# Local layers: feed forward's first product in fp32r parts, and norms without a power

## The chip, the cores and the metric

The kernel runs on one core of a Trainium2 chip. The metric is the device time of one execution in microseconds (us). The core's engines are named as the profile names them: PE (TensorE), ACT (ScalarE), DVE (VectorE), POOL (GpSimd) and SP (SyncE, which here only issues DMAs). Each runs its own list of instructions in order, and they wait for one another on semaphores.

## The reference, cut to what matters

The reference has four parts: an attention with relative positions, six local layers, a second attention, and a mixture of experts. The change touches the six local layers. A batch has 16 sequences of 256 tokens with 128 channels, and per layer this is computed (after the first 64 channels are kept and the other 64 are shifted by one token):

```python
qkv = x @ Wqkv                       # 16 heads of 64
q = q / max(norm(q), 1e-12) * q_scale;  k likewise
q, k = rotary(q, k)                  # cos, sin and a scale for each position
out = local_attention(q, k, v)       # windows of 32 tokens, QK_SCALE 8
x = out @ Wo + x
xn = (x - mu) / sqrt(var + 1e-5) * g + bln     # on the shifted x
a, gate = split(xn @ W1 + b1)        # W1 is 128 x 682
x = (a * gelu(gate)) @ W2 + b2 + x
```

## The kernel before

The local layers are one block of five instruction lists (lines 1253 to 2106). For each layer and each sequence there is a pass (`one_pass`) of four steps, numbered 0 to 3; a step is 128 tokens and eight heads (`s % 2` chooses the tokens, `s // 2` the heads). 6 layers x 16 sequences are 96 passes and 384 steps. The lists are software pipelined by hand. In step j of pass n:

- PE projects q and k of step j+4 (`project_qk`), transposes the normed q and k of step j+2 (`turn_qk`), projects v of j+4, transposes outputs (`turn_outputs`, L1579) and probabilities (`turn_probs`, L1593), computes the scores of j+2 (L1612), multiplies by Wo (L1631) and by the values (L1641).
- ACT does the exponentials of step j+1 (L1821), writes the mask into the score banks (L1825), squares q and k of j+4 (L1798), and copies transposed tiles out of PSUM.
- DVE multiplies q and k of j+4 by the rotation tables (L1943 to L1945, `t_done`), sums the squares (L1950), subtracts the maxima from the scores (L1966, `sub_done`), then takes the floor of the sums (L1956, `floor_done`), and norms the outputs.
- POOL runs `normalise_rows`: it adds the two halves of the rotation (L1416), raises the 128x16 sums to -0.5 (L1420), and multiplies (L1427, `qk_done`).

The feed forward of the sequence before, f = n - 1, is laid into the same pass. In step 0 DVE takes its moments and POOL its deviations (`deviations`, L1433 to L1438, between the power and the multiplication of step 0). At the end of step 1 PE transposes the normed input (`turn_xn`, L1652) and ACT applies gain and shift to it (`turned_xn`, L1837). In step 2 PE runs `first_gates` just behind `project_v`, and `last_gate_and_value` behind the scores; in step 3 it runs `first_values`. Each of the three is a call of `through_w1` (L1658): two chunks of W1 as stationary operand, at most 128 columns of it, with the 256 tokens moving. These products are in fp32, which the trace shows as two instructions each; the products with Wqkv are already in fp32r, three products of rounded parts for one.

POOL also prepares what the passes need: after `normalise_rows` of step 1 it splits the x of the sequence after the next into two rounded parts (`split_x`, L1444 and L1447, for `turn_x`), and in the last passes of a layer it makes the low parts of the next Wqkv (`low_part`, L1410). In `first_gates` PE waits for `xnT_done`, which ACT raises at L1837. A table of ACT functions is loaded twice a pass: for Gelu in step 2 (a Gelu of one column, L1793, makes the load come early), and for Exp in step 3 (L1821).

Of the kernel before, what the change touches and what calls it, by code (L numbers as in the profile page):

```python
# [18 lines left out]
F32 = mybir.dt.float32  # L19
# [6 lines left out]
P = 128  # L26
# [31 lines left out]
def shape_constants():  # L58
# [39 lines left out]
    c["rot_cos"] = lay(cos * scale * f(8), cos * inv)  # L98
    c["rot_sin"] = lay(sin * scale * f(8), sin * inv)
# [32 lines left out]
def build_program(nc, T, out):  # L132
    ctx = ExitStack()
    with ctx:
# [106 lines left out]
        with ExitStack() as st:  # L241
# [42 lines left out]
            ev_wr, tabs = sem("a_ev_wr"), sem("a_tabs")  # L284
# [6 lines left out]
            ROW, EXT, PRODUCT, PP, CHAIN = 2, 3, 4, 5, 6  # L291
            E_HIGH, E_LOW, EK_MASKED, EK_HIGH, EK_LOW = 6, 7, 8, 9, 11

            x_copied, queries_ok = sem("a_x_copied"), sem("a_queries_ok")
            far = sem("a_far")
# [6 lines left out]
            with nc.Block() as block:  # L302
                @block.sync
                def _(sp):
# [6 lines left out]
                    for name, t in (("L0_attn_Ek", 1), ("L0_attn_Eq", 2)):  # L311
# [12 lines left out]
                    sp.dma_start(tab_ext.rearrange("t d r -> d t r"), ext[:, 0:2, :]).then_inc(tabs, 16)  # L324
                    sp.wait_ge(tabs, 16)
                    sp.dma_start(ek_row, bass.AP(tab_ext, HD * NREX + KREV,
                                                 [[0, P // HD], [NREX, HD], [1, KJ]])).then_inc(tabs, 16)
                    sp.dma_start(eq_tab[:, :], bass.AP(tab_ext, 0, [[1, LB], [NREX, HD], [1, TABW]])).then_inc(tabs, 16)
                    sp.wait_ge(tabs, 16 * 3)
# [3 lines left out]
                def _(act):  # L333
# [6 lines left out]
                    for t in range(LT):  # L340
                        act.dma_start(e_col[:, t:t + 1], bass.AP(T["L0_attn_Eq"].tensor, t * (NREL - 1) * HD,
                                                                 [[0, P // HD], [1, HD], [1, 1]]),
                                      allow_slow_non_contiguous=True).then_inc(far, 16)
                        row = (1 - t) * (NREL - 1)
                        act.dma_start(ev_far[:, t, :], T["L0_attn_Ev"][row:row + 1, :].broadcast_to((P, HD))
                                      ).then_inc(far, 16)
# [8 lines left out]
                def _(pool):  # L355
# [11 lines left out]
                    pool.wait_ge(far, 16 * 2 * LT)  # L367
# [7 lines left out]
                    pool.wait_ge(ld_w, 48)  # L375
# [7 lines left out]
                    pool.wait_ge(tabs, 16 * 3)  # L383
# [773 lines left out]
        with ExitStack() as st:  # L1157
# [9 lines left out]
            w1 = sb(st, "b_w1", [P, 2 * FF])  # L1167
            w2 = sb(st, "b_w2", [P, 3, D])
# [8 lines left out]
            rnorm = sb(st, "b_rnorm", [P, 2, 16])  # L1177
            t1, t2 = sb(st, "b_t1", [P, 2, 16, BD]), sb(st, "b_t2", [P, 2, 16, BD])
# [45 lines left out]
            masked = sem("b_masked")  # L1224

            N_WA, N_LN, N_W1, N_W2 = 3, 2, 5, 3
            SEQ = 4
# [29 lines left out]
            with nc.Block() as block:  # L1257
# [148 lines left out]
                def _(pool):  # L1406
# [6 lines left out]
                    def normalise_rows(n, s, deviations_of=None):  # L1413
# [17 lines left out]
                    def deviations(f):  # L1431
# [6 lines left out]
                        nc.gpsimd.tensor_tensor(shift[:, :], less_mean[:, :], frstd[:, :], ALU.mult).then_inc(shift_done, 1)  # L1438

# [20 lines left out]
                    def one_pass(l, b, front=True, ffn=True, last_front=False, new_front=False, x_follows=True,  # L1460
                                 last_norm=False):
# [24 lines left out]
                    nc.gpsimd.memset(zero[:, :], 0.0)  # L1486
                    nc.gpsimd.memset(ss_floor[:, :, :, 1], 1e-24).then_inc(filled, 1)
# [11 lines left out]
                    one_pass(0, 1, last_norm=True)  # L1499
                    for l in range(DEPTH - 1):  # L1500
# [5 lines left out]
                        one_pass(l + 1, 1)  # L1506
# [4 lines left out]
                    deviations(DEPTH * B - 1)  # L1511

                @block.tensor
                def _(pe):
# [24 lines left out]
                    def by_high(r, s, i, new_layer):  # L1539
                        hg, ts = s % SEQ // 2, slice(s % 2 * P, s % 2 * P + P)  # L1540
                        if new_layer is not None and s % 2 == 0:

                            pe.wait_ge(w_low, new_layer * 6 + (3 * hg + i + 1))
# [216 lines left out]
                def _(act):  # L1760
                    def load_projections(l):

                        act.wait_ge(w_low, l * 6)
# [58 lines left out]

                    def mask(s):
# [22 lines left out]
                    def one_pass(part, l, b, x_follows=True, ffn=True, last_front=False, new_ffn=None):  # L1846
# [45 lines left out]
                    act.wait_ge(c_ld, 96)  # L1892
                    one_pass("first", 0, 0, ffn=False)
# [964 lines left out]
```

## Time and profile before

| | us |
|---|---|
| median of three runs (5007.28 to 5029.31) | 5020.37 |
| the profiled execution | 5004.04 |
| its span | 5002.2 |
| PE busy | 4560.0 (91%) |
| PE weight loads busy | 3754.4 (75%) |
| DVE busy | 3696.6 (74%) |
| ACT busy | 3399.6 (68%) |
| POOL busy | 3558.5 (71%) |
| mean granted clock of PE, share of full speed | 0.972 |

The span runs from the first to the last instruction. The local layers fill it from about 970 us to 4230 us. A busy share is an average over parts of the kernel with different limits, so the order of events inside one pass says more than the share.

### The profile page before, as it was taken

What the parts mean: (1) busy time and instruction counts of PE and PEld (TensorE: products, weight loads), DVE (VectorE), ACT (ScalarE), POOL (GpSimd) and SP (SyncE); (2) the same over time, 40 slices, a digit from 0 to 9 for tenths busy, and PEclk for the clock granted to TensorE, in tenths of its full rate; (3) what the DMA queues carried; (4) which work ended last, traced back from release to release, by engine and by line L of the source; (5) the groups of instructions that cost most, each with busy time, mean ns of one, the idle gap of its engine ahead of it and who ended that gap; (6) DMA issues with size and microseconds to landing.
All of it is one profiled execution on the core that took longest, in us unless ns stands there. A gap on an engine that the chain in (4) does not pass through costs nothing. (4 is left out here: it accounts for less than half of the span.)

```text
span 5002.2 us, 202509 instructions
## 1 busy us (share of the span) xinstructions
PE 4560.0 (91%) x82160; PEld 3754.4 (75%) x82160; DVE 3696.6 (74%) x7406; ACT 3399.6 (68%) x6468; POOL 3558.5 (71%) x2507
## 2 busy tenths in 40 slices
PE   6888888799999999999999999999999997888879
PEld 4777777678887888788877887888877885555557
DVE  4877777788887888778877888788877884555544
ACT  3565565577777777777777777777777774666664
POOL 3334334499999999989999999999999995222212
PEclk8999999999999999999999999999999998999889
DMA  4333333332223222332223222322232221000000
GB/s 119 98 101 112 98 104 105 93 84 69 68 69 88 70 68 69 73 83 69 69 72 85 70 69 70 87 69 70 68 74 70 69 68 40 1 0 0 0 1 18
DMA packets 500471, 338.98 MB, mean 68 GB/s; under 512 B 222559, under 2 KB 489084, under 8 KB 499213
## 3 DMA queue, kind: packets, MB, share of 16 engines
q1 hardware_dynamic: 493566, 320.55, 25.3%
q10 hardware_dynamic: 6544, 13.18, 0.9%
q8 instruction: 280, 4.59, 0.4%
q14 instruction: 81, 0.66, 0.0%
HBM read 60.06 MB, written 54.58 MB: 23 GB/s over the span
## 5 line engine op out<-in xcount | busy, mean ns | idle before, releaser
L1420 POOL TENSOR_TENSOR b_rnorm<-b_ss,neghalf 128x16 f32<-128x16 f32 x384 | 1118.2, 2912 | 25.1 <-DVE b_ss L1956 21.5
L1416 POOL TENSOR_TENSOR b_rot<-b_t 128x1024 f32<-128x1024 f32 x384 | 909.5, 2369 | 75.3 <-DVE b_t L1945 74.6
L1943 DVE TENSOR_TENSOR b_t<-psum,b_cosg 128x1024 f32<-128x1024 f32 x384 | 469.6, 1223 | 426.3 <-ACT b_sq L1798 420.3
L1427 POOL TENSOR_TENSOR b_qk<-b_rot,b_rnorm 128x1024 f32<-128x1024 f32 x384 | 731.0, 1904 | 42.8 <-POOL b_rnorm L1420 2.7
L1544 PE MATMUL psum<-b_w_hi,b_xT_parts 128*128 128x512 f32 x1152 | 528.0, 458 | 28.6 <-issue 19.3
L1798 ACT ACTIVATE b_sq<-psum 128x1024 f32<-128x1024 f32 x384 | 392.1, 1021 | 221.9 <-PE psum L1549 221.5
L1950 DVE TENSOR_REDUCE b_ss_floor<-b_sq 128x16 f32<-128x1024 f32 x384 | 464.3, 1209 | 0.0
L1549 PE MATMUL psum<-b_w_hi,b_xT_parts 128*128 128x512 f32 x1152 | 459.9, 399 | 0.0
L1545 PE MATMUL psum<-b_w_lo,b_xT_parts 128*128 128x512 f32 x1152 | 457.3, 397 | 0.0
L1631 PE MATMUL psum<-shared,b_oT 128*128 128x128 f32 x3072 | 425.2, 281 | 0.8 <-ACT b_oT L1816 0.8
L1533 PE MATMUL psum<-ident,b_qk 128*128 128x128 f32 x3072 | 405.9, 275 | 21.3 <-DVE b_o L1982 15.3
L1533 PEld LDWEIGHTS psum<-ident,b_qk 128*128 128x128 f32 x3072 | 360.0, 142 | 84.9 <-DVE b_o L1982 25.7
L1631 PEld LDWEIGHTS psum<-shared,b_oT 128*128 128x128 f32 x3072 | 380.0, 191 | 27.2 <-issue 1.5
L1821 ACT ACTIVATE b_pr<-b_pr 128x512 f32<-128x512 f32 x384 | 241.6, 629 | 217.0 <-DVE b_pr L1966 197.2
L1982 DVE TENSOR_TENSOR b_o<-psum,b_rs 128x256 f32<-128x256 f32 x768 | 326.2, 425 | 26.5
L1641 PE MATMUL psum<-b_v_win,b_prT 64*32 64x65 f32 x24576 | 336.4, 225 | 3.9 <-issue 3.8
L1612 PE MATMUL psum<-b_kT,b_qTs 64*32 64x64 f32 x24576 | 333.3, 224 | 0.4 <-issue 0.4
L1658 PE MATMUL psum<-b_xnT,b_w 128*128 128x256 f32 (+1 forms) x1152 | 306.2, 388 | 16.8 <-DVE b_hid L2006 2.9
L1612 PEld LDWEIGHTS psum<-b_kT,b_qTs 64*32 64x32 f32 x24576 | 270.6, 105 | 61.5 <-issue 49.4
L1641 PEld LDWEIGHTS psum<-b_v_win,b_prT 64*32 64x32 f32 x24576 | 272.1, 105 | 51.5 <-issue 5.0
L1816 ACT COPY b_oT<-psum 128x512 f32<-128x512 f32 x384 | 232.5, 605 | 112.6 <-PE psum L1579 112.5
L2357 ACT ACTIVATE c_probs<-psum,c_nmax 128x256 f32<-128x256 f32 x512 | 200.9, 482 | 117.5 <-DVE c_nmax L2424 117.2
(271 smaller groups left out, 11545.8 us busy)
## 6 DMA issues: line engine op xcount, KB each, us to landing
b_v_win<-b_v SPq DMA_DIRECT2D x2304, 65.0 KB
keyed<-shared SPq DMA_DIRECT2D x64, 768.0 KB, 4.7
b_v_win<-b_v SPq DMA_DIRECT2D x1152, 32.5 KB
a_logits<-keyed SPq DMA_DIRECT2D x128, 160.0 KB, 3.1
oa<-XR SPq DMA_DIRECT2D x1024, 2.0 KB
xcur<-X SPq DMA_DIRECT2D x111, 128.0 KB, 4.3
shared<-in_L_ffn_Wqkv_dram ACTq DMA_DIRECT2D x6, 1536.0 KB
a_logits<-keyed SPq DMA_DIRECT2D x64, 128.0 KB, 3.0
```

The source lines that it names most:

```text
L1416: nc.gpsimd.tensor_tensor(rot[:, i, :, :], t1[:, i, :, :], t2[:, i, :, :], ALU.add).then_inc(rot_done, 1)
L1420: nc.gpsimd.tensor_tensor(rnorm[:, i, :], ss[:, i, :], neghalf[:, :], ALU.pow).then_inc(rn_done, 1)
L1427: nc.gpsimd.tensor_tensor(qk[:, i, :, :], rot[:, i, :, :], rnorm[:, i, :, None].broadcast_to((P, 16, BD)), ALU.mult).then_inc(qk_done, 1)
L1533: last = nc.tensor.transpose(r[:, p * P:(p + 1) * P], qk[:, s % 2, a * 8 + 2 * p:a * 8 + 2 * p + 2, :].rearrange("p h d -> p (h d)"), iden ...
L1544: nc.tensor.matmul(r, xT_hi[:, ts], w_hi[:, piece(hg, i)], start=True, stop=False)
L1545: nc.tensor.matmul(r, xT_hi[:, ts], w_lo[:, piece(hg, i)], start=False, stop=False)
L1549: return nc.tensor.matmul(r, xT_lo[:, ts], w_hi[:, piece(hg, i)], start=False, stop=True)
L1612: last = nc.tensor.matmul(bank[3 + j][qs, p * 2 * WIN:(p + 1) * 2 * WIN], qTs[at, p, qs], kT[at, p, keys], start=False, stop=(p == 3), ski ...
L1631: last = nc.tensor.matmul(bank_c[:, 0:D], oT[:, p, :], wo[:, 4 * (s % SEQ // 2) + p, :], start=(p == 0), stop=(p == 3))
L1641: last = nc.tensor.matmul(r[qs, p * (BD + 1):(p + 1) * (BD + 1)], prT[at, p, qs], v_win[at, s % NV, c, p, :], start=(p == 0), stop=(p == 3 ...
L1943: nc.vector.tensor_tensor(t14, x4, tab(cosg, slice(0, BD), BD), ALU.mult)
L1950: nc.vector.tensor_reduce(ss_floor[:, t, :, 0], sq[:, :].rearrange("p (h d) -> p h d", d=BD), AX.X, ALU.add).then_inc(ss_done, 1)
```

## The change

Four edits go together.

1. `through_w1` multiplies in fp32r: W1 is split into `w1_hi` and `w1_lo`, the normed input into `xn_parts[0]` (high) and `xn_parts[1]` (low), and each chunk is hi x hi + lo x hi + hi x low. A last chunk of 85 columns is computed as 86.
2. The parts are made thus. ACT writes the high part beside `xnT` in `turned_xn`, a second 128x256 activation. POOL subtracts it for the low part (`split_xn`), at the head of step 2, before that step's `normalise_rows`, and PE waits for it (`xn_split`) in `first_gates`. W1 is split once a layer on POOL (`split_w1`) behind `split_x` in step 1 of the second pass of the layer.
3. The power at L1420 goes. ACT takes the logarithm of the sums and the exponential of -0.5 times it (`guess_norms`, between the exponentials and the mask). POOL makes one Newton step of it: four tensor_tensors of 128x16, each behind the one before. The factor 0.5 is in the rotation tables.
4. ACT preloads a table set that has both functions, in step 3 of each pass; some semaphores of the set-up are merged.

```diff
@@ constants
-    c["rot_cos"] = lay(cos * scale * f(8), cos * inv)
-    c["rot_sin"] = lay(sin * scale * f(8), sin * inv)
+    c["rot_cos"] = lay(cos * scale * f(4), cos * inv * f(0.5))
+    c["rot_sin"] = lay(sin * scale * f(4), sin * inv * f(0.5))
@@ POOL, normalise_rows
-                        pool.wait_ge(floor_done, m)
-                        nc.gpsimd.tensor_tensor(rnorm[:, i, :], ss[:, i, :], neghalf[:, :],
-                                                ALU.pow).then_inc(rn_done, 1)
+                        pool.wait_ge(guess_done, 2 * m)
+                        nc.gpsimd.tensor_tensor(rn_step[:, i, :], ss[:, i, :], rn_guess[:, i, :], ALU.mult).then_inc(step_done, 1)
+                        pool.wait_ge(step_done, 3 * m - 2)
+                        nc.gpsimd.tensor_tensor(rn_step[:, i, :], rn_step[:, i, :], rn_guess[:, i, :], ALU.mult).then_inc(step_done, 1)
+                        pool.wait_ge(step_done, 3 * m - 1)
+                        nc.gpsimd.tensor_tensor(rn_step[:, i, :], three[:, :], rn_step[:, i, :], ALU.subtract).then_inc(step_done, 1)
+                        pool.wait_ge(step_done, 3 * m)
+                        nc.gpsimd.tensor_tensor(rnorm[:, i, :], rn_step[:, i, :], rn_guess[:, i, :], ALU.mult).then_inc(rn_done, 1)
@@ POOL, new
+                    def split_xn(f):
+                        pool.wait_ge(xnT_done, 2 * f + 2)
+                        nc.gpsimd.tensor_tensor(xn_parts[:, 1, :], xnT[:, :], xn_parts[:, 0, :].bitcast(F32),
+                                                ALU.subtract).then_inc(xn_split, 1)
+
+                    def split_w1(l):
+
+                        both = slice(0, 2 * FF)
+                        pool.wait_ge(w1_ld, (l + 1) * (16 * N_W1))
+                        nc.gpsimd.tensor_tensor(w1_hi[:, both], w1[:, :], ones[:, 0:1].broadcast_to((P, 2 * FF)),
+                                                ALU.mult).then_inc(w_low, 1)
+                        pool.wait_ge(w_low, l * N_LOW + 7)
+                        nc.gpsimd.tensor_tensor(w1_lo[:, both], w1[:, :], w1_hi[:, both].bitcast(F32),
+                                                ALU.subtract).then_inc(w_low, 1)
@@ POOL, one_pass
                         for s in range(SEQ):
+                            if ffn and s == 2:
+                                split_xn(n - 1)
                             if front:
                                 normalise_rows(n + 1, s, n - 1 if ffn and s == 0 else None)
                             if last_front and s == 0:
                                 layer_gains(l + 1)
                             if x_follows and s == 1:
                                 split_x(n + 2)
+                            if new_ffn and s == 1:
+                                split_w1(l)
@@ PE
-                            last = nc.tensor.matmul(ffn_bank[0:w, j * S:(j + 1) * S], w1[:, k:k + w], xnT[:, :],
-                                                    start=(j == 0), stop=(j == 1), skip_group_check=True)
+                            w += w % 2
+                            for i, (weight, part) in enumerate(((w1_hi, 0), (w1_lo, 0), (w1_hi, 1))):
+                                last = nc.tensor.matmul(ffn_bank[0:w, j * S:(j + 1) * S], weight[:, k:k + w],
+                                                        xn_parts[:, part, :], start=(j == 0 and i == 0),
+                                                        stop=(j == 1 and i == 2), skip_group_check=True)
@@ PE, first_gates
-                            pe.wait_ge(w1_ld, (new_ffn + 1) * (16 * N_W1))
-                        pe.wait_ge(xnT_done, f + 1)
+                            pe.wait_ge(w_low, (new_ffn + 1) * N_LOW)
+                        pe.wait_ge(xn_split, f + 1)
@@ ACT
+                    def guess_norms(s, m):
+
+                        i = s % 2
+                        act.wait_ge(floor_done, m)
+                        nc.scalar.activation(log_ss[:, i, :], ss[:, i, :], ACT.Ln).then_inc(guess_done, 1)
+                        act.wait_ge(guess_done, 2 * m - 1)
+                        nc.scalar.activation(rn_guess[:, i, :], log_ss[:, i, :], ACT.Exp, scale=-0.5).then_inc(guess_done, 1)
@@ ACT, turned_xn
                         nc.scalar.activation(xnT[:, :], ffn_bank[:, 0:S], ACT.Identity, bias=lnb[:, 0:1],
                                              scale=lng[:, 0:1]).then_inc(xnT_done, 1)
+                        nc.scalar.activation(xn_parts[:, 0, :], ffn_bank[:, 0:S], ACT.Identity, bias=lnb[:, 0:1],
+                                             scale=lng[:, 0:1]).then_inc(xnT_done, 1)
@@ ACT, one_pass
+                            if j == 3 and ffn:
+                                nc.scalar.preload_act_table_set(LOG_EXP)
                             if ok(j + 1):
                                 exps(j + 1, m + 1)
+                            if ok(j + 3):
+                                guess_norms(j + 3, m + 3)
```

## Rows read from the trace of the kernel before

**Rows 1.** Busy time of each engine in a steady stretch: PE, weight loads, DVE, ACT, POOL, clock, DMA.

```profile
2200.00:2300.00 100.00, 97.81 (x2034) 82.05 (x2033) 81.74 (x177) 75.46 (x131) 94.42 (x55) 1.00 0.28 69
```

**Rows 2.** Timeline of PE, end of step 1 and step 2: start, us, engine, line, operands.

```profile
2222.00 0.44 PE L1652 MATMUL psum<-ident,b_xn 128*128 128x128 f32 x2
...
2225.25 1.03 PE L1658 MATMUL psum<-b_xnT,b_w 128*128 128x256 f32 x4
2226.52 0.66 PE L1579 MATMUL psum<-ident,b_o 128*128 128x128 f32 x4 [0.24 <-ACT b_qTs L1785]
2227.01 0.81 PE L1593 MATMUL psum<-ident,b_pr 128*128 128x128 f32 x4
2227.76 0.86 PE L1612 MATMUL psum<-b_kT,b_qTs 64*32 64x64 f32 x64
2228.75 1.09 PE L1658 MATMUL psum<-b_xnT,b_w 128*85 128x256 f32 x4
...
2231.46 0.50 PE L1544 MATMUL psum<-b_w_hi,b_xT_parts 128*128 128x512 f32 x1
```

**Rows 3.** Timeline of DVE, rotation of step 1 and floor of its sums.

```profile
2219.59 0.68 DVE L1945 TENSOR_TENSOR b_t<-psum,b_sing 128x512 f32<-128x512 f32 x1
...
2222.64 0.17 DVE L1956 TENSOR_REDUCE b_ss<-b_ss_floor 128x16 f32<-128x32 f32 x1
```

**Rows 4.** Timeline of POOL in the same stretch.

```profile
2219.02 0.19 POOL L1438 TENSOR_TENSOR b_shift<-b_less_mean,b_frstd 128x2 f32<-128x2 f32 x1
2219.17 1.90 POOL L1427 TENSOR_TENSOR b_qk<-b_rot,b_rnorm 128x1024 f32<-128x1024 f32 x1
2221.03 2.38 POOL L1416 TENSOR_TENSOR b_rot<-b_t 128x1024 f32<-128x1024 f32 x1
2223.36 2.92 POOL L1420 TENSOR_TENSOR b_rnorm<-b_ss,neghalf 128x16 f32<-128x16 f32 x1
2226.42 1.90 POOL L1427 TENSOR_TENSOR b_qk<-b_rot,b_rnorm 128x1024 f32<-128x1024 f32 x1
2228.28 0.61 POOL L1444 TENSOR_TENSOR b_x_parts<-xcur,ones 128x256 fp32r<-128x256 f32 x1
2228.97 0.73 POOL L1447 TENSOR_TENSOR b_x_parts<-xcur,b_x_parts 128x256 fp32r<-128x256 f32 x1
```

**Rows 5.** Timeline of ACT in the same stretch.

```profile
2222.48 0.56 ACT L1837 ACTIVATE b_xnT<-psum,b_lnb,b_lng 128x256 f32<-128x256 f32 x1 [1.56 <-PE psum L1652]
2222.94 0.62 ACT L1821 ACTIVATE b_pr<-b_pr 128x512 f32<-128x512 f32 x1
2223.58 1.28 ACT L1793 ACT_TABLE_LOAD   x1
2224.87 0.20 ACT L1793 ACTIVATE b_no_gate<-ones 128x1 f32<-128x1 f32 x1
```

**Rows 6.** Timeline of PE in the first attention: fp32r products of 256 columns.

```profile
500.94 0.28 PE L654 MATMUL psum<-a_k_diag,a_e_parts 128*128 128x256 f32 x1
501.06 0.28 PE L650 MATMUL psum<-a_k_diag,a_q_parts 128*128 128x256 f32 x1
```

**Rows 7.** Timeline of PE: stalls at L1652, idle time in brackets; first, third and last of eight.

```profile
1514.53 0.41 PE L1652 MATMUL psum<-ident,b_xn 128*128 128x128 f32 x2 [4.24 <-ACT b_xn L1832]
...
2154.25 0.69 PE L1652 MATMUL psum<-ident,b_xn 128*128 128x128 f32 x2 [3.50 <-ACT b_xn L1832]
...
4192.60 0.41 PE L1652 MATMUL psum<-ident,b_xn 128*128 128x128 f32 x2 [2.50 <-ACT b_xn L1832]
```

**Rows 8.** Busy time and granted clock (last but two) around these three stalls.

```profile
1513.00:1523.00 10.00, 8.47 (x100) 7.11 (x101) 4.35 (x6) 8.08 (x15) 9.78 (x7) 0.83 0.35 87
2150.00:2160.00 10.00, 6.50 (x82) 5.16 (x80) 6.93 (x19) 4.69 (x8) 7.91 (x7) 0.67 0.33 82
...
4190.00:4200.00 10.00, 6.74 (x100) 5.31 (x90) 2.77 (x11) 5.53 (x10) 1.19 (x4) 0.83 0.38 75
```

**Rows 9.** Waits of PE: who waited for whom, us in total, times, longest.

```profile
PE psum L1652 <- ACT b_xn L1832: 41.7, 19, 7.6
```

More of the change, by code:

```diff
@@ L283, in build_program @@
             ld_x, ld_c, ld_w, ld_e = sem("a_ld_x"), sem("a_ld_c"), sem("a_ld_w"), sem("a_ld_e")
-            ev_wr, tabs = sem("a_ev_wr"), sem("a_tabs")
+            ev_wr = sem("a_ev_wr")
             ev_row = k_blk[0:1, :, :].rearrange("p h l -> p (h l)")[:, 0:NREX * HD]
@@ L291, in build_program @@
             ROW, EXT, PRODUCT, PP, CHAIN = 2, 3, 4, 5, 6
+            TURNED, TABLES = 4, 6
             E_HIGH, E_LOW, EK_MASKED, EK_HIGH, EK_LOW = 6, 7, 8, 9, 11
             x_copied, queries_ok = sem("a_x_copied"), sem("a_queries_ok")
-            far = sem("a_far")
             def window_blocks(mt, hh):
@@ L323, in _ @@
                     sp.wait_ge(made, EXT)
-                    sp.dma_start(tab_ext.rearrange("t d r -> d t r"), ext[:, 0:2, :]).then_inc(tabs, 16)
-                    sp.wait_ge(tabs, 16)
+                    sp.dma_start(tab_ext.rearrange("t d r -> d t r"), ext[:, 0:2, :]).then_inc(ld_e, 16)
+                    sp.wait_ge(ld_e, 16 * TURNED)
                     sp.dma_start(ek_row, bass.AP(tab_ext, HD * NREX + KREV,
-                                                 [[0, P // HD], [NREX, HD], [1, KJ]])).then_inc(tabs, 16)
-                    sp.dma_start(eq_tab[:, :], bass.AP(tab_ext, 0, [[1, LB], [NREX, HD], [1, TABW]])).then_inc(tabs, 16)
-                    sp.wait_ge(tabs, 16 * 3)
+                                                 [[0, P // HD], [NREX, HD], [1, KJ]])).then_inc(ld_e, 16)
+                    sp.dma_start(eq_tab[:, :], bass.AP(tab_ext, 0, [[1, LB], [NREX, HD], [1, TABW]])).then_inc(ld_e, 16)
+                    sp.wait_ge(ld_e, 16 * TABLES)
                     sp.wait_ge(ld_x, 16)
@@ L342, in _ @@
                                                                  [[0, P // HD], [1, HD], [1, 1]]),
-                                      allow_slow_non_contiguous=True).then_inc(far, 16)
+                                      allow_slow_non_contiguous=True).then_inc(ld_w, 16)
                         row = (1 - t) * (NREL - 1)
                         act.dma_start(ev_far[:, t, :], T["L0_attn_Ev"][row:row + 1, :].broadcast_to((P, HD))
-                                      ).then_inc(far, 16)
+                                      ).then_inc(ld_w, 16)
                     act.dma_start(X[:, :, :], x_in).then_inc(ld_x, 16)
@@ L366, in _ @@
                     nc.gpsimd.memset(v_far[:, :, :, :, :], 1.0)
-                    pool.wait_ge(far, 16 * 2 * LT)
+                    pool.wait_ge(ld_w, 16 * (3 + 2 * LT))
                     low = slice(2 * GC, P)
@@ L374, in _ @@
                     pool.wait_ge(set_ok, E_LOW)
-                    pool.wait_ge(ld_w, 48)
                     for w, rep in ((wq, wq_rep), (wk, wk_rep)):
@@ L382, in _ @@
                     pool.wait_ge(ld_c, 16 * 6)
-                    pool.wait_ge(tabs, 16 * 3)
+                    pool.wait_ge(ld_e, 16 * TABLES)
                     nc.gpsimd.tensor_tensor(ek_masked, ek_row[:, None, :].broadcast_to((P, 4, KJ)),
@@ L1167, in build_program @@
             w1 = sb(st, "b_w1", [P, 2 * FF])
+            w1_hi, w1_lo = sb(st, "b_w1_hi", [P, 2 * FF + 2], F32R), sb(st, "b_w1_lo", [P, 2 * FF + 2], F32R)
+            xn_parts = sb(st, "b_xn_parts", [P, 2, S], F32R)
             w2 = sb(st, "b_w2", [P, 3, D])
@@ L1177, in build_program @@
             rnorm = sb(st, "b_rnorm", [P, 2, 16])
+            log_ss, rn_guess, rn_step = (sb(st, f"b_{n}", [P, 2, 16]) for n in ("log_ss", "rn_guess", "rn_step"))
+            three = sb(st, "b_three", [P, 16])
             t1, t2 = sb(st, "b_t1", [P, 2, 16, BD]), sb(st, "b_t2", [P, 2, 16, BD])
@@ L1223, in build_program @@
             gel_done, hid_done = sem("b_gel_done"), sem("b_hid_done")
-            masked = sem("b_masked")
+            masked, xn_split = sem("b_masked"), sem("b_xn_split")
+            guess_done, step_done = sem("b_guess_done"), sem("b_step_done")
+            LOG_EXP = "natural_log_exp_and_others"
             N_WA, N_LN, N_W1, N_W2 = 3, 2, 5, 3
+            N_LOW = 6 + 2
             SEQ = 4
@@ L1486, in _ @@
                     nc.gpsimd.memset(zero[:, :], 0.0)
+                    for parts in (w1_hi, w1_lo):
+                        nc.gpsimd.tensor_tensor(parts[:, 2 * FF:], ones[:, 0:2], ones[:, 0:2], ALU.subtract)
+                    nc.gpsimd.memset(three[:, :], 3.0)
                     nc.gpsimd.memset(ss_floor[:, :, :, 1], 1e-24).then_inc(filled, 1)
@@ L1498, in _ @@
                     one_pass(0, 0, ffn=False)
-                    one_pass(0, 1, last_norm=True)
+                    one_pass(0, 1, last_norm=True, new_ffn=True)
                     for l in range(DEPTH - 1):
@@ L1505, in _ @@
                         one_pass(l + 1, 0)
-                        one_pass(l + 1, 1)
+                        one_pass(l + 1, 1, new_ffn=True)
                     with pool.Fori(2, B - 2) as b:
@@ L1511, in _ @@
                     deviations(DEPTH * B - 1)
+                    split_xn(DEPTH * B - 1)
                 @block.tensor
@@ L1761, in load_projections @@
                     def load_projections(l):
-                        act.wait_ge(w_low, l * 6)
+                        act.wait_ge(w_low, l * N_LOW)
                         act.wait_ge(gains, l * 6)
@@ L1892, in _ @@
                     act.wait_ge(c_ld, 96)
+                    nc.scalar.preload_act_table_set(LOG_EXP)
                     one_pass("first", 0, 0, ffn=False)
```

4 lines of the change are left out of this document (2 added, 2 removed).

## The prediction

> **What bounds the kernel now.** I read the busy shares of a steady stretch of the local layers first. A pass takes 33 us (96 of them in some 3200 us). PE is busy 97.8 of 100 us at full clock, POOL 94.4 us, ACT 75.5 us [rows 1]. So PE sets the pace there and POOL is close behind it. Next I read the timelines of PE, DVE, POOL and ACT over one step, because the change moves work between engines and adds a wait, and a share cannot price a wait. The reader is to see there how far POOL runs behind PE: when PE starts the first gates at 2225.25 [rows 2], POOL is still in the step before. It ends the split of x, the last thing that it does in step 1, at 2228.97 + 0.73 = 2229.70 [rows 4]. That costs nothing now, since PE asks for the q and k of this step only two steps later. Last I read PE's stalls and what the granted clock did after them [rows 7, 8].
>
> **The change, part by part.**
>
> *Products.* Four instructions of the first gates take 2226.28 - 2225.25 = 1.03 us with their tail, and the next rows start 0.86 us apart where nothing waits; I take 0.86 / 4 = 0.215 us each, and there are 12 a pass, 2.58 us [rows 2]. An fp32r product of 256 columns starts 0.12 us after the one before [rows 6]. 18 of them are 2.16 us. PE sheds 0.42 us a pass. The 86th column and the wider stationary operand are nothing beside it, since the moving side sets the distance.
>
> *Power against guess and Newton step.* POOL loses 2.92 us a step [rows 4]. Four tensor_tensors of 128x16 come in. The trace has 0.19 us for 128x2 and 0.61 for 128x256 [rows 4], so 128x16 is 0.2 us, plus 0.1 us for each wait on the one before (0.14 us lies between the end of the power and the next row): 4 x 0.3 = 1.2 us, with bounds of 0.8 and 2.8 us. On ACT, Ln and Exp of 128x16 lie between 0.20 us (one column) and 0.62 (512 columns) [rows 5]; I take 0.25 each with the wait, 0.5 us a step. ACT has a quarter of its time free [rows 1], so by itself this is nothing.
>
> *The new wait, which decides.* The low part of xn is made on POOL at the head of step 2, so behind the whole of `normalise_rows` and `split_x` of step 1 in POOL's list. PE waits for it in `first_gates`, at the front of step 2, with everything else of the step queued behind: output and probability transposes, scores, Wo and values. I follow the chain with the times of this pass.
> - PE's transposes of xn start at 2222.00 and end at 2222.44 [rows 2]. ACT's `xnT` starts at 2222.48. The high part is a second one, and the next instruction started 0.46 us after it: 2222.94 to 2223.40. The exponentials, which began at 2222.94, begin at 2223.40 and end at 2224.0 [rows 5]. The floor of the sums is there since 2222.81 [rows 3]. Ln and Exp end at about 2224.5.
> - POOL has ended the rotation's sum at 2221.03 + 2.38 = 2223.4, which needs no less time now: it starts behind the q and k of step 0, and these behind the deviations at 2219.17 [rows 4], which wait for DVE's moments and not for the power. Newton step from 2224.5 to 2225.75; multiplication from 2225.85 (it began at 2226.42). From its start to the end of `split_x` the rows show 2229.70 - 2226.42 = 3.28 us, so 2229.1. `split_xn` is a subtraction of 128x256 like the 0.73 us one: 2229.85, and 0.1 to PE: 2229.95.
> - PE would be there at 2225.25. The stall is 4.7 us. Only 0.6 us of the 1.7 that POOL sheds reach this point, as the guess comes from ACT late.
>
> Bounds: were the guess free of any wait and the rotation's sum started when DVE is done (2219.59 + 0.68 = 2220.27 [rows 3]), it would be 0.1 + 2.4 + 0.8 + 0.1 + 3.28 + 0.73 + 0.1: 2227.8, a stall of 2.5 us. With 2.8 us for the Newton step and 1.2 for the guess it would be 7.0 us.
>
> *What the stall hides.* While PE stands, ACT, which was late in this step, catches up. So three short waits of step 2 go: 0.24 us before the output transposes, 0.26 in those of the probabilities (0.75 us to the next row, against 0.49 for the four output transposes of the same shape), 0.13 behind the scores, 0.63 in all [rows 2]. Net of it and the products: 4.7 - 0.63 - 0.42 = 3.6 us a pass, 2.5 to 7.0 less 1.1 at the bounds. 94 of 96 passes have this order: 338 us.
>
> *The clock.* Eight stalls of 2.5 us or more at L1652 stand in the local layers between 1514 and 4193 us, each followed by a stretch at half the clock (1.2 instead of 2.4 GHz): the mean over ten us is 0.83 in four and 0.66 or 0.67 in the other four [rows 7, 8]. That is 3.4 us or 6.7 us at 0.5. What PE loses is half of what lies behind the stall: in the case at 2154.25 the mean of 0.67 up to 2160 leaves nearly all that follows the stall at half, some 5.8 us, so 3 us are lost; where the stretch is short, 1.7 us or less. I take 2.2 us, and nine passes of ten: 94 x 2.0 = 188 us. Bounds: 0 and 3.0 a pass.
>
> The Trainium skill, "TensorE: Matmul & The Clock Gate" (HAM oscillation), speaks against this change: bursts of products with waits between them send the array to half rate again and again, once for every wait. The rows agree for eight single stalls. With that rule the term is paid in every pass, without it the sum would be 188 us less.
>
> *Layer changes.* PE's waits at L1652 are 41.7 us [rows 9]; some 30 of them come from POOL being late with the low parts of Wqkv, and a lighter POOL returns most, with the clock of eight stalls, 8 x 2.2 = 18 us. Against that `split_w1` (128x682, by width 1.6 + 1.9 us) stands before `split_xn` in six passes, 21 us, and two low parts of 128x512 (1.2 to 1.5 us each by width) in five, 13 us. Together -14 us. The first passes, where PE waits for POOL's q and k, and the chain at the end cancel to within 5 us. Set-up semaphores and tables of constants: nothing, as no instruction is added.
>
> *Sum.* 338 + 188 - 14 = 512 us on the profiled execution, 5004.0 (its span 5002.2 and 1.8 around it): 5516. The three runs shown have their median 16 us above that execution, and their lowest 3 us above it. I round to 5510.
>
> **Rivals.**
>
> *A. POOL is in time, and PE's savings show* (faster). POOL sheds 1.7 us a step or about 7 us a pass of 33; if its lead over PE grew with that, the low part would be there at 2225.25. Then 94 x (0.42 + 0.24) = 62 us and some 40 at the layer changes come back: 4900. It decides from the point where POOL ends `split_x` 4.5 us earlier. Against it: step 1 cannot start on POOL before DVE's rotation at 2220.27, and that comes from PE's own projection. No lead can be built up.
>
> *B. The stall is there, the clock mostly is not.* The clock may stay up after some of the stalls, or the stall may be near its lower bound: 94 x (3.6 + 0.4) - 14 gives 5366; with a stall of 3.2 us and falls in half of the passes 94 x (2.1 + 1.1): 5290. For it: eight cases are few, and the bound of 2.5 us lies at the shortest of them. Against it: no long stall is without a fall [rows 7, 8].
>
> *C. Table loads.* If Ln and Exp came from different sets, each step would load two more tables, 2 x 1.28 us [rows 5], on ACT's 24.9 us a pass: 24.9 + 10.3 + 2.5 = 37.7 us of work, with its waits above 42, and the guess 2.6 us later, so the stall 7.3: 5004 + 94 x 9.5 = 5900. Against it: the preload names one set for both.
>
> The Trainium skill, "ScalarE: Activation LUTs" (Table sets: the hidden batching unit), lists a set with exp and ln, one load for both. By it C does not occur; no row here shows it.
>
> **How the numbers follow.** The forecast (5400 to 5630) has 0.66; B (5200 to 5400) 0.18; A 0.08; C and longer stalls 0.05; a small slowdown below 5200 0.03. The range that leaves out two in ten is 5270 to 5640. What a measurement can tell from no change is about 0.5%, 25 us. Faster by more than that is A without its smallest gains, 0.07; within it 0.03; slower 0.90.
>
> **What would show it.** In the trace after: L1658's first row of a pass begins some 4.7 us after PE's last projection of v, with POOL's subtraction named as releaser, about 94 times and some 440 us in total; the pass is 38 to 39 us instead of 33; the granted clock of the local layers falls from 1.00 to near 0.9; POOL's busy share falls below 75%; rows of L1658 start 0.12 us apart; two table loads a pass. Wrong would be: no idle time before the first gates, or idle time there and a clock at 1.00 throughout, or more than two loads a pass.

## The result: 9% slower, by a stall once a pass, and the profile after

The changed kernel takes 5469.96 us (median of four runs, 5467.92 to 5473.10) against 5019.01 us before, a ratio of 1.09 with a 95% interval of 1.0875 to 1.0925. The forecast was 5510, its range 5270 to 5640. One execution of all that this text uses, of e5 below, ran far slower (7815.8 us at a mean clock of 0.84) and is left out of its ratio.

The page of the profile after, its first part, and below it a stretch that answers to [rows 1], and that holds two passes just behind one with a new W1 (busy time of PE, weight loads, DVE, ACT, POOL, then clock and DMA):

```profile
PE 4659.0 (85%) x82736; PEld 3899.7 (71%) x82736; DVE 3703.2 (68%) x7406; ACT 3596.7 (66%) x7335; POOL 2879.3 (53%) x3770
```

```profile
2300.00:2400.00 100.00, 85.83 (x1716) 73.04 (x1714) 72.09 (x153) 69.01 (x134) 64.12 (x86) 0.93 0.28 75
```

PE was busy 97.8 of 100 us and is busy 85.8. POOL fell from 94.4 to 64.1, as it was meant to, and nothing came of it. Every engine is now idler than before, and such a picture calls for a chain of waits. PE's waits name it (who waited for whom: us in total, times, longest us):

```profile
PE psum L1700 <- POOL b_xn_parts L1458: 431.7, 96, 7.3
...
PE psum L1692 <- ACT b_xn L1883: 16.8, 12, 6.8
```

L1700 is `through_w1` and L1458 the subtraction in `split_xn`: 96 waits, 432 us, where the same products waited for POOL not once before. The waits that [rows 9] counted as 41.7 us are 16.8. The timeline of PE through step 2, against [rows 2]:

```profile
2314.77 0.43 PE L1692 MATMUL psum<-ident,b_xn 128*128 128x128 f32 x2
...
2317.77 0.40 PE L1589 MATMUL psum<-b_w_hi,b_xT_parts 128*128 128x512 f32 x1
2322.49 0.58 PE L1700 MATMUL psum<-b_xn_parts,b_w_hi 128*128 128x256 f32 x1 [4.33 <-POOL b_xn_parts L1458]
...
2323.94 1.05 PE L1619 MATMUL psum<-ident,b_o 128*128 128x128 f32 x4
2324.79 1.06 PE L1633 MATMUL psum<-ident,b_pr 128*128 128x128 f32 x4
2325.78 1.19 PE L1652 MATMUL psum<-b_kT,b_qTs 64*32 64x64 f32 x64
2326.89 0.51 PE L1700 MATMUL psum<-b_xn_parts,b_w_hi 128*86 128x256 f32 x1
...
2333.07 0.28 PE L1700 MATMUL psum<-b_xn_parts,b_w_hi 128*128 128x256 f32 x1
2333.18 0.28 PE L1700 MATMUL psum<-b_xn_parts,b_w_lo 128*128 128x256 f32 x1
```

The reader sees 4.33 us of idle time at 2322.49. Behind it four transpositions take 1.05 us that take 0.66 in [rows 2]: PE runs at half its clock. At full clock, at 2333.07, a product of the new kind starts 0.11 us after the one before.

The timeline of POOL in that stretch shows the chain that PE waited for, against [rows 4]:

```profile
2311.84 1.90 POOL L1443 TENSOR_TENSOR b_qk<-b_rot,b_rnorm 128x1024 f32<-128x1024 f32 x1
2313.71 2.38 POOL L1427 TENSOR_TENSOR b_rot<-b_t 128x1024 f32<-128x1024 f32 x1
2317.21 0.22 POOL L1431 TENSOR_TENSOR b_rn_step<-b_ss,b_rn_guess 128x16 f32<-128x16 f32 x1 [1.13 <-ACT b_rn_guess L1872]
...
2318.11 0.22 POOL L1437 TENSOR_TENSOR b_rnorm<-b_rn_step,b_rn_guess 128x16 f32<-128x16 f32 x1
2318.47 1.90 POOL L1443 TENSOR_TENSOR b_qk<-b_rot,b_rnorm 128x1024 f32<-128x1024 f32 x1
2320.33 0.62 POOL L1475 TENSOR_TENSOR b_x_parts<-xcur,ones 128x256 fp32r<-128x256 f32 x1
2321.02 0.73 POOL L1478 TENSOR_TENSOR b_x_parts<-xcur,b_x_parts 128x256 fp32r<-128x256 f32 x1
2321.71 0.73 POOL L1458 TENSOR_TENSOR b_xn_parts<-b_xnT,b_xn_parts 128x256 fp32r<-128x256 f32 x1
```

And the timeline of ACT, against [rows 5]:

```profile
2315.24 0.56 ACT L1888 ACTIVATE b_xnT<-psum,b_lnb,b_lng 128x256 f32<-128x256 f32 x1 [1.56 <-PE psum L1692]
2315.71 0.56 ACT L1890 ACTIVATE b_xn_parts<-psum,b_lnb,b_lng 128x256 fp32r<-128x256 f32 x1
2316.16 0.62 ACT L1864 ACTIVATE b_pr<-b_pr 128x512 f32<-128x512 f32 x1
2316.68 0.21 ACT L1870 ACTIVATE b_log_ss<-b_ss 128x16 f32<-128x16 f32 x1
2316.92 0.22 ACT L1872 ACTIVATE b_rn_guess<-b_log_ss 128x16 f32<-128x16 f32 x1
2317.15 1.28 ACT L1836 ACT_TABLE_LOAD   x1
2318.45 0.20 ACT L1836 ACTIVATE b_no_gate<-ones 128x1 f32<-128x1 f32 x1
```

The high part exists at 2316.27, two microseconds before PE wants the low part. POOL stands idle from 2316.1 to 2317.2 with the subtraction further down in its list. The clock around the stall (last but two), against [rows 8], then in a stall of the steady passes and in the ten us behind it, and last over the local layers:

```profile
2320.00:2330.00 10.00, 7.51 (x156) 6.80 (x156) 4.61 (x7) 5.09 (x10) 4.68 (x5) 0.66 0.28 73
...
2469.76:2474.08 4.32, 0.00 (x0) 0.00 (x1) 2.90 (x4) 3.34 (x7) 4.10 (x6) 1.00 0.18 47
2474.08:2484.08 10.00, 10.00 (x177) 8.85 (x178) 4.57 (x11) 7.00 (x13) 4.12 (x6) 0.83 0.18 47
...
980.00:4180.00 3200.00, 2774.32 (x56672) 2367.20 (x56671) 2269.89 (x4849) 2252.57 (x4374) 2047.37 (x2655) 0.94 0.25 64
```

The long fall at 2320 is the rarer case. In the steady passes the clock is full through nearly all of the stall, falls just behind it, and 3.4 us are granted at half (0.83 over ten us). Counted pass by pass, each of the 96 stalls has a fall behind it, and of the 422 us at half clock up to the last pass 58 lie inside a stall and 364 behind one.

### The profile page after: what moved, and what is told of

Its sections match the earlier page's. It is cut to its first block and busy times, and to the rows that moved or that the text cites. A ratio compares the mean times of both kernels' runs of the same rounds, so it can differ in the third digit from the quotient of the medians.

```text
span 5468.3 us, 207085 instructions
## 1 busy us (share of the span) xinstructions
PE 4659.0 (85%) x82736; PEld 3899.7 (71%) x82736; DVE 3703.2 (68%) x7406; ACT 3596.7 (66%) x7335; POOL 2879.3 (53%) x3770
## 5 line engine op out<-in xcount | busy, mean ns | idle before, releaser
L1700 PE MATMUL psum<-b_xn_parts,b_w_hi 128*128 128x256 f32 (+1 forms) x1152 | 319.7, 337 | 435.5 <-POOL b_xn_parts L1458 431.7
L1700 PEld LDWEIGHTS psum<-b_xn_parts,b_w_hi 128*128 128x128 f32 (+1 forms) x1152 | 222.6, 210 | 494.2 <-POOL b_xn_parts L1458 429.5
L1431 POOL TENSOR_TENSOR b_rn_step<-b_ss,b_rn_guess 128x16 f32<-128x16 f32 x384 | 85.3, 222 | 832.1 <-ACT b_rn_guess L1872 832.1
L2020 DVE TENSOR_REDUCE b_m_own<-psum 128x8 f32<-128x512 f32 x384 | 262.3, 683 | 367.6 <-PE psum L1652 366.7
L1896 ACT ACTIVATE b_gel<-psum,b_b 128x256 f32<-128x256 f32 (+1 forms) x288 | 125.5, 469 | 396.1 <-PE psum L1700 396.1
L1652 PE MATMUL psum<-b_kT,b_qTs 64*32 64x64 f32 x24576 | 353.6, 238 | 1.1 <-issue 1.1
L1652 PEld LDWEIGHTS psum<-b_kT,b_qTs 64*32 64x32 f32 x24576 | 286.5, 113 | 80.7 <-issue 80.2
```

The costliest lines, as they stand in the source:

```text
L1652: last = nc.tensor.matmul(bank[3 + j][qs, p * 2 * WIN:(p + 1) * 2 * WIN], qTs[at, p, qs], kT[at, p, keys], start=False, stop=(p == 3), ski ...
L1700: last = nc.tensor.matmul(ffn_bank[0:w, j * S:(j + 1) * S], weight[:, k:k + w], xn_parts[:, part, :], start=(j == 0 and i == 0), stop=(j = ...
```

## The experiments

All start from the changed kernel unless the text says otherwise, and all are compared with the kernel before. Each ratio is to executions of the kernel before that were taken beside the run: their median was 5006.7 us for e1, e2, e3 and e5, and 5012.3 for the others, against the 5019.0 of the first comparison. The changed kernel was measured in the first comparison alone, so a difference between it and an experiment is uncertain by some 10 us. "Pass" is the distance between two starts of ACT's `xnT` row, in the steady part of the stretch from 2220 to 2520 us, and for e4 in the middle of each layer. The times for the kernel before, e1, e5 to e7 and e9 to e11 are means.

| kernel | median us | ratio to before (95% interval) | pass, us |
|---|---|---|---|
| before | 5019.0 | | 32.86 |
| changed | 5470.0 | 1.09 (1.0875 to 1.0925) | 37.5 |
| e1 low part made in step 1 | 5074.1 | 1.0135 (1.0117 to 1.0153) | 33.42 |
| e2 low part ahead of `split_x` | 5288.2 | 1.0552 (1.0523 to 1.0581) | 34.8 to 37.4 |
| e3 PE kept busy in the stall | 5374.1 | 1.0736 (1.0714 to 1.0758) | 36.1 |
| e4 power kept | 5593.3 | 1.1163 (1.1145 to 1.1182) | 38.0 to 39.5 |
| e5 Newton step alone | 5028.1 | 1.0036 (1.0023 to 1.0048) | 33.26 |
| e6 as e1, power kept | 5082.8 | 1.0145 (1.0128 to 1.0162) | 33.04 |
| e7 as e1, high part on POOL, W1 split earlier | 5016.1 | 1.0012 (1.0001 to 1.0022) | 32.96 |
| e9 as e7, ACT's list reordered, one power | 5012.1 | 1.0001 (0.9991 to 1.0011) | 32.85 |
| e10 as e9, mask on DVE | 4975.8 | 0.9926 (0.9908 to 0.9945) | 32.32 |
| e11 before, mask on DVE | 4994.2 | 0.9969 (0.9957 to 0.9981) | 32.53 |

**e1: is it the place of the subtraction, or the added work?** Only its place in POOL's list is changed, into the gap before the Newton step.

```diff
                         nc.gpsimd.tensor_tensor(rot[:, i, :, :], t1[:, i, :, :], t2[:, i, :, :], ALU.add)...
+                        if split_of is not None:            # n - 1 in step 1
+                            split_xn(split_of)
...
-                            if ffn and s == 2:
+                            if ffn and s == 2 and not front:   # the last pass keeps the old place
                                 split_xn(n - 1)
```

> Only the place of split_xn on POOL is changed: from behind split_x of step 1 to between the sum of the rotation and the Newton step of step 1, where POOL waits 1.13 us for the guess in the changed kernel. Theory (the stall is made by what stands before split_xn in POOL's list): the 4.33 us before the first gates go, the granted clock returns to about 0.99 in the local layers. The six passes with a new W1 keep a wait of some 6.5 us on its low part. ACT is late in step 2 by 0.8 us more than in the kernel before, so I expect PE's wait for the copied q of 0.24 us to become about 1.1 us a pass. Time 5004 + 94 x 0.45 us and the layer changes: 5000 to 5070. Rival (what costs time is the added work on ACT and POOL as a whole, not its place): the time stays above 5350.

5074 us, 4 above the theory's range and far below the rival's 5350. All instructions of the change are there and 396 of its 451 us are gone. PE's waits in the trace of e1:

```profile
PE psum L1622 <- ACT b_qTs L1831: 96.3, 91, 1.2
PE psum L1703 <- POOL b_w_lo L1470: 38.6, 6, 6.5
...
PE psum L1703 <- POOL b_xn_parts L1460: 5.1, 7, 1.9
```

The stall is gone from the steady passes. In its place PE waits for the copied q once a pass, 1.2 us where [rows 2] have 0.24, since ACT got the high part and the guess in front of it. The pass adds up: 32.85 - 0.42 + (1.22 - 0.24) = 33.4 us. With the subtraction in the gap the change costs 1.35%; its place in the list was worth the rest.

**e2: does the stall follow the list?**

```diff
-                            if ffn and s == 2:
+                            if ffn and s == 2 and not x_follows:
                                 split_xn(n - 1)
...
+                            if ffn and s == 1 and x_follows:
+                                split_xn(n - 1)
...
                             if x_follows and s == 1:
                                 split_x(n + 2)
```

> split_xn is put just ahead of split_x in step 1, behind the multiplication of q and k. It comes 1.38 us earlier. Theory: the stall shrinks from 4.33 to 2.95 us, 94 x 1.38 = 130 us less, 5340; the clock still falls in most passes. If stalls of 3 us no longer bring the clock down, it is 5340 less up to 94 x 1.5, that is down to 5200. Rival (the stall comes from the guess alone): no change, 5470.

PE's waits, and the steady case in its timeline:

```profile
PE psum L1702 <- POOL b_xn_parts L1458: 259.7, 90, 3.5
PE psum L1702 <- POOL b_w_lo L1468: 41.1, 6, 7.3
```

```profile
2335.64 0.58 PE L1702 MATMUL psum<-b_xn_parts,b_w_hi 128*128 128x256 f32 x1 [2.96 <-POOL b_xn_parts L1458]
```

2.96 us against 4.33, within a hundredth what leaving out `split_x` gives. The time is 182 us less and not 130. The waits account for 131: the 431.7 us before hold the six long stalls of the passes with a new W1, which stand here in the second row, so 259.7 + 41.1 = 300.8 us is what they compare with. The remaining 51 us (34 between the two profiled executions) are put down to the clock, which falls in 69 of the 96 passes and not in all; 332 us of the local layers are at half clock against 422.

The same trace prices the fall. Three passes close to one another have the same stall. The clock (last but two) stays up in the first row, falls in the second, and falls for twice as long in the third (windows of one pass each, from one stall to the next):

```profile
2479.69:2514.53 34.84, 31.60 (x680) 27.11 (x680) 27.19 (x58) 26.60 (x53) 23.72 (x32) 1.00 0.26 65
2443.58:2479.69 36.11, 32.87 (x680) 28.17 (x680) 27.19 (x58) 26.70 (x53) 23.71 (x32) 0.95 0.25 63
2332.68:2370.05 37.37, 34.11 (x680) 29.35 (x680) 27.20 (x58) 26.81 (x53) 23.73 (x32) 0.91 0.24 61
```

Over the ten middle passes of each layer the means are 34.8 us (17 passes), 36.2 us with 3.4 us at half clock (28) and 37.3 us with 6.8 (15). So 3.4 us at half clock make a pass 1.4 us longer, and 6.8 us 2.5.

**e3: what does the halved clock cost by itself?** The stall keeps its place and length, except in the six passes with a new W1, but PE computes something through it.

```diff
                         if new_ffn is not None:
                             pe.wait_ge(w_low, (new_ffn + 1) * N_LOW)
+                        pe.wait_ge(xnT_done, 2 * f + 2)
+                        for _ in range(20):
+                            nc.tensor.matmul(ffn_bank[:, 0:P], ident[:, :], ident[:, :], start=True, stop=True)
                         pe.wait_ge(xn_split, f + 1)
```

> The changed kernel, with 20 fp32 transposition-size products (128 columns, about 4.3 us) of the identity put before the wait for the low part, so that PE works through the stall. The place and length of the stall stay. Theory (a stall costs its length and then the halved clock): granted clock about 1.00 in the local layers, pass about 36 us, time 5250 to 5340, that is 130 to 220 us less than 5470. Rival (the halved clock costs nothing, since other engines set the time after a stall): 5450 to 5480.

Timeline of PE in a pass with a new W1 and in one behind it, and the local layers, in the trace of e3:

```profile
2247.15 7.51 PE L1710 MATMUL psum<-ident 128*128 128x128 f32 x40 [6.08 <-POOL b_w_lo L1468]
...
2324.55 4.63 PE L1710 MATMUL psum<-ident 128*128 128x128 f32 x40
2328.93 0.36 PE L1700 MATMUL psum<-b_xn_parts,b_w_hi 128*128 128x256 f32 x1
```

```profile
980.00:4180.00 3200.00, 3099.26 (x61630) 2717.34 (x61631) 2332.65 (x4983) 2298.38 (x4490) 2103.64 (x2728) 0.99 0.26 66
```

The clock stays up (0.99 against 0.94), the first gates begin 4.38 us late as before, and 96 us are gone, where I wrote down 130 to 220 beforehand. The 96 are a net figure. In the six passes with a new W1 the twenty products stand behind PE's wait for it and do not cover it, and they take 7.51 us where PE has just stood for 6.08. By the traces these passes are 24 us longer together than in the changed kernel, and the others 117 us shorter, 1.3 each on average and 1.4 in the steady stretch (37.5 to 36.1), the same as e2 shows. And the pass of 36.1 us is the stall's own cost made visible: 4.33 - 0.42 - 0.63 = 3.28 us over 32.86. The passes of e2 with no fall agree: 2.96 - 0.42 - 0.63 = 1.91 us over 32.86 are 34.8.

**e4: power kept, products changed.** (The normalisation lines of the diff are undone, with Ln, Exp and the preload.)

> Only the products are changed: fp32r parts, split_xn at the head of step 2 as in the changed kernel; the norms are by the power on POOL as before, nothing of Ln and Exp on ACT. Theory (PE waits for POOL's list up to split_xn): in the kernel before POOL ended split_x 4.45 us after PE came to the first gates; 0.73 us for the low part and 0.1 more make a stall of 5.2 to 5.4 us against 4.33, so 94 x 0.9 us = 85 us above the changed kernel, and the stalls of the layer changes come back: 5540 to 5620. Rival (Ln and Exp on ACT make the stall): the stall is shorter than 4.33 us and the time below 5470.

PE's waits:

```profile
PE psum L1695 <- POOL b_xn_parts L1453: 520.8, 96, 9.8
```

89 us more of waiting than in the changed kernel, 85 were computed; 5593 us, inside the range. The sum is right in part by luck: the steady stall is 4.94 us where 5.2 to 5.4 were expected, so it grew by 0.6 us and not 0.9, and the rest of the waiting came near the layer changes. More of the time is at half clock, too (0.92 over the local layers, against 0.94). So the Newton step had shortened the stall from 4.94 to 4.33 us and no more: its guess comes late from ACT.

**e5: Newton step alone, fp32 products.** (The products, the splits and the second activation are undone.)

> Feed forward's product as before (fp32, W1 not split, no low part, no second activation); the norms by logarithm, exponential and Newton step stay. Theory: no stall before the first gates. Ln and Exp delay ACT by 0.5 us in step 2, so PE's wait for the copied q grows from 0.24 to about 0.7 us a pass, 43 us in all; a lighter POOL gives back the stalls at layer changes and their clock, 45 us. 4990 to 5020. Rival (POOL set the pace together with PE): 4900 to 4960.

PE's waits:

```profile
PE psum L1614 <- ACT b_qTs L1820: 56.5, 100, 1.0
PE psum L1687 <- ACT b_xn L1875: 25.3, 14, 8.1
```

5028 us, 0.36% slower, and the rival (POOL sets the pace too) is out: POOL is unloaded from 94 to 69 us of 100 and the kernel doesn't gain. The wait for q is 0.6 us where it was 0.25, and the pass 0.4 us longer; Ln and Exp put 0.46 us in front of it. My 4990 to 5020 was a little low.

**e6: e1 with the power.** (e4 and e1 together.)

> As e1 (split_xn in step 1, between rotation and norm), but with the power on POOL as before and no Ln or Exp on ACT. Theory (ACT's list in step 2 sets the pace once the stall is gone): without the 0.47 us of Ln and Exp PE's wait for the copied q falls from 1.22 to about 0.75 us, but POOL has 31.8 us of work in a pass of 33 and its stalls at the layer changes stay or grow: pass 32.9 to 33.1 us, 5030 to 5090. Rival (POOL would be the bound with the power): pass above 33.5 us, over 5110.

```profile
PE psum L1617 <- ACT b_qTs L1826: 62.9, 82, 0.9
PE psum L1698 <- POOL b_w_lo L1465: 50.7, 6, 9.7
PE psum L1690 <- ACT b_xn L1881: 42.6, 19, 8.1
```

The pass is 0.4 us shorter than in e1, ACT's part, and what that gains is lost at the layer changes, where POOL is late (50.7 + 42.6 us against 38.6 + 18.1). With the subtraction in its gap, power and Newton step come out within 9 us of each other.

**e7: less on ACT.** (e1, with the high part made on POOL, and W1 split behind step 0.)

```diff
-                        nc.scalar.activation(xn_parts[:, 0, :], ffn_bank[:, 0:S], ACT.Identity, ...)
+                        nc.gpsimd.tensor_tensor(xn_parts[:, 0, :], xnT[:, :], ones[:, 0:1].broadcast_to((P, S)), ALU.mult)...
-                            if new_ffn and s == 1:
+                            if new_ffn and s == 0:
                                 split_w1(l)
```

> e1 with two more moves: the high part of xn is made on POOL (128x256, 0.6 us) in place of the second activation on ACT, and W1 is split behind step 0 instead of behind step 1. Theory: ACT's list in step 2 is 0.46 us shorter, PE's wait for the copied q falls from 1.22 to 0.76 us, pass 33.4 to 32.95 us (43 us); the six waits for W1's low part of 6.4 us fall to 2 us, with the clock of some of them (30 us): 4990 to 5015. Rival (the wait for the copied q comes from the table load alone): no change of the pass, 5040.

```profile
PE psum L1625 <- ACT b_qTs L1834: 60.1, 83, 1.0
PE psum L1706 <- POOL b_xn_parts L1463: 29.0, 18, 2.7
```

Pass 32.96, as computed, and 5016 us, 1 above the range: level with the kernel before, to 0.1%.

**e9: the same work on ACT in another order, and one guess less.**

```diff
-                            nc.scalar.activation(no_gate[:, :], ones[:, 0:1], ACT.Gelu)   # before the squares
...
                                 mask(j + 2)
+                                nc.scalar.activation(no_gate[:, :], ones[:, 0:1], ACT.Gelu)
...                              # v is copied behind the two Gelus; in step 1 POOL makes the norm by
+                            nc.gpsimd.tensor_tensor(rn_step[:, i, :], ss[:, i, :], neghalf[:, :], ALU.pow)...
+                            nc.gpsimd.tensor_tensor(rnorm[:, i, :], rn_step[:, i, :], rn_step[:, i, :], ALU.add)...
```

> e7 with ACT's list of step 2 shortened ahead of the copied q: the Gelu table is loaded behind the mask instead of before the squares, v is copied behind the two Gelus, and the norm whose guess falls into step 2 is made by the power on POOL (2.9 us, and one addition for the factor of two), the other three by the Newton step. Theory: q is copied before PE asks for it, the wait of 0.76 us goes and some 0.3 us come up before the second gates and Wo instead; pass 32.2 to 32.6 us, 4925 to 4970, the first version faster than the kernel before. Rival (ACT's work from the turned xn to the copied probabilities sets step 2 in whatever order): pass 32.9, 4990 to 5010.

```profile
PE psum L1712 <- ACT b_gel L1903: 61.6, 79, 0.9
PE psum L1712 <- POOL b_xn_parts L1469: 36.6, 18, 2.7
```

A miss of 40 us: 5012. The wait for q went, and a wait of up to 0.9 us for the Gelus stands in its place. This is what the rival says: ACT's work from the turned xn to the copied probabilities must be done before PE can go on, in whatever order it stands.

**e10 and e11: so take work off ACT.** DVE is idle there and writes the mask of step 2. e11 is this edit alone in the kernel before.

```diff
+                            if j == 2 and ffn and ok(j + 2):
+                                dve.wait_ge(sub_done, m + 1)
+                                nc.vector.tensor_copy(scored..., masks...).then_inc(masked, 1)
...                              # and on ACT
-                            if ok(j + 2) and gates_follow:
-                                mask(j + 2)
```

> e9, and the mask of step 2 (a copy of 128x512 into the score banks, 0.5 us of ACT's list between the copied k and the Gelu table) is written by DVE, which stands idle before the rotation of step 2. Theory (ACT's work between the turned xn and the copied probabilities of step 2 sets the length of that step, in whatever order it stands): 0.5 us less work there is 0.4 to 0.5 us less a pass, 32.35 us, 4960 to 4980, 0.7 to 1.0% faster than the kernel before. Rival (PE is the bound at 32.8 us): no change from 5012.

> The kernel before with this one edit alone: the mask of step 2 written by DVE. There ACT's mask stands behind the copied k, so the wait for the copied q (0.24 us) stays, and what goes is the wait of the transposed probabilities for the mask and that for the Gelus, 0.26 and 0.13 us a pass: 32.85 to 32.5 us, 4970 to 4990. If the gain is as large as or larger than that of e10 over e9, fp32r parts and the Newton step are worth nothing on top of it; by the theory e10 is below e11 by 0.1 to 0.2 us a pass, 10 to 20 us. Rival: e11 is at or below e10.

PE's wait for the Gelus in e10:

```profile
PE psum L1712 <- ACT b_gel L1903: 24.2, 62, 0.9
```

61.6 us of waiting became 24.2, the pass 32.3 us, the kernel 4976 us: 0.74% faster than before (interval 0.55 to 0.92%), and the fastest version here. e11 is 4994, 0.3% faster and 4 us above its range. The intervals don't meet, so all that e10 has beyond the mask, the fp32r parts and Newton steps with the new places and orders of e9, is worth about 0.4%, 18 us. No run separates these parts.

## Why the prediction was right, step by step

*The bound.* PE at 98% and a chain read from timelines and not from shares: right. By shares alone this change relieves the second busiest engine.

*Products.* 0.42 us a pass were computed; the first values took 0.86 us before and take 0.70 now (2333.07 to 2333.77), 0.47 for three such calls.

*Newton step and guess.* 1.2 us were taken for the Newton step: from 2317.21 to 2318.33 it is 1.12. Half a microsecond for Ln and Exp: 0.46. The guess arrives late and takes back part of what the power's removal gave, as the 1.13 us of idle time before L1431 shows.

*The stall.* 4.7 us were computed, 4.33 measured in the steady pass, 431.7 in total against some 440. Counted from the transpositions of xn, the low part comes 0.2 us earlier than computed: PE starts 0.05 us behind the subtraction and not 0.1, the split's rows lie closer, and guess and Newton step are a little shorter. The other 0.14 us is how the profile counts: idle time begins at the end of the row before (2318.17), where the prediction took the start that the next row would have had. e2 shortens it by the computed amount, e4 lengthens it by 0.6 us, less than the 0.9 computed, and e1 removes it. This is shown, not argued.

*What the stall hides.* 0.63 us. It was not measured by itself: what e3's pass and the e2 passes without a fall confirm, to 0.05 us, is the sum of stall, products and this term.

*The clock.* The term that was mis-sized: 2.0 us a pass and 188 in all were written down. e2 and e3 measure 1.4 in a steady pass, some 130 us over 94 passes. That the clock falls was right, and it falls in every pass. Two things in the price were wrong. First, the mean of 2.2 us was taken over eight stalls of which four had the long fall; of the 60 middle passes here 58 have the short one, 3.4 us. Second, PE was charged half of all that lies behind the stall, 1.7 us for 3.4, and the trace shows 1.4. Why is in part in the rows. PE at full clock in the trace of e3, against 2323.94 to 2326.89 above:

```profile
2438.11 0.60 PE L1619 MATMUL psum<-ident,b_o 128*128 128x128 f32 x4
2438.55 0.60 PE L1633 MATMUL psum<-ident,b_pr 128*128 128x128 f32 x4
2439.08 0.86 PE L1652 MATMUL psum<-b_kT,b_qTs 64*32 64x64 f32 x64
2439.86 0.35 PE L1700 MATMUL psum<-b_xn_parts,b_w_hi 128*86 128x256 f32 x1
```

From start to start the transpositions nearly double at half clock (0.44 to 0.85 us), but the 64 score products take 1.11 us against 0.78, 1.4 times as long.

The Trainium skill, "TensorE: Matmul & The Clock Gate" (HAM oscillation), advises an order of the products in which the array does not stand between bursts. Its picture of a fall for every wait is what the trace shows here, and e3, where PE does not stand, agrees (0.99 against 0.94 with the same 4.4 us). The size had to come from the runs.

*Layer changes.* -14 us were taken. The waits at L1692 fell by 25 us, and the six passes with a new W1 stall 6.85 us instead of 4.3, 15 us more in all. The local layers grew by 454 us, and 95 times the 4.7 us of a steady pass are 446, so the layer changes cost some 8 us where 14 were to come back: small, as taken, with the other sign.

*Sum.* 4.33 - 0.42 - 0.63 = 3.28 us for the stall and 1.4 for the clock make 4.7 us, and times 94 that is 440 of the 451 us measured. The forecast looks closer than its terms were. 512 us were added to one execution of 5004.0 us, 15 us below the median before, and 5516 was rounded down. Against the 451 measured the growth was 61 us too large: some 56 are the clock's and 30 the stall's, and some 25 come back because the layer changes cost about 11 us and did not give 14. The 40 us between 5510 and 5470 are in part luck.

*What would show it.* The wait, its releaser and its total, POOL's share, the distance of 0.11 us and two table loads a pass came as written. The pass is 37.5 us and not 38 to 39, and the clock 0.94 and not near 0.9, both by the smaller clock term.

*Rivals.* A is out: no lead of POOL was built up, and e5 shows that its relief is worth nothing by itself. B is out too: the clock stayed up behind none of the 96 stalls. The time lies between B and the forecast because a fall costs less than was taken. C is out: two loads a pass. The Trainium skill, "ScalarE: Activation LUTs" (What ACT_TABLE_LOAD costs), puts a change of set at about 2.7 us, a load of 1.28 and a drain of about as much. Here the load takes 1.28 us, the activation before it ended 0.01 us ahead and the next starts 0.02 us after it, so on this path the measured 1.3 us is the price.

## What to carry to other kernels

A step that is made cheaper helps only as far as its inputs come earlier, and a new product of a busy engine costs what stands before it in that engine's list; place it by the time at which its consumer asks and the time at which its input is there (here a gap of 1.1 us was free, and 396 of 451 us hung on it). Put the whole of a pass's chain on paper for the engine that bounds it before adding a wait there, and count a stall there with the clock that falls behind it (here 1.4 us on top of 3.3). When reordering an engine's list only moves the wait, as in e9, the list is too long: take work off it.

## What the runs showed of the hardware that was not expected

Keeping PE busy with twenty idle products through a stall of 4.4 us kept its clock at 0.99 and made the kernel 96 us faster (e3), with nothing useful computed. Stalls of 3 us bring the clock down as well, but not each time: in 69 of 96 passes in e2, where 4.3 us did it in all 96. With the same stall before it, 3.4 us at half clock cost 1.4 us and 6.8 us cost 2.5, less than half of their length (e2). Ln and Exp of 128x16 on ACT take 0.21 and 0.22 us and need no table load between them, and a tensor_tensor of 128x16 on POOL takes 0.22 us, against 2.9 for the power of the same shape.
